# Score tiles of the maxima cut to 64 queries, the masked quarter left out, and the maxima turned by one transposition

## The reference

```python
# local attention: 16 heads of 16; a query sees only keys before it (distance 1..128)
allowed = (dist > 0) & (dist <= w) & (k_gpos >= 0)
scores = where(allowed, einsum('bhnqd,bhnkd->bhnqk', qb, kb) * scale, NEG)
local = softmax(scores) @ v            # rows with no allowed key give 0
# ... plus latent attention over 64 pooled tokens, a gate, and an output projection
# cross attention: 16 heads of 16, keys and values from ctx, causal (key <= query)
q, k, v = relu(query @ Wq + bq), relu(key @ Wk + bk), relu(value @ Wv + bv)
scores = where(tril, q k^T / sqrt(16), NEG)
out = layer_norm(softmax(scores) @ v + q) * gamma + beta
```

## Time and profile before

| | |
|---|---|
| median of three runs | 1628.79 us (1628.71 to 1629.89) |
| the profiled execution | 1626.49 us |
| its span, first to last instruction | 1624.8 us |
| PE busy | 1518.2 us (93%) |
| DVE, ACT, POOL busy | 1153.4 (71%), 931.4 (57%), 874.4 (54%) us |
| local attention, cross attention, slots | about 20 to 735, 735 to 1310, 1310 to 1625 us |

### The profile page before, as it was taken

The page is one execution under the profiler, slowest core; times in us unless marked ns, Lnnn a source line. Parts: engine busy times, 40 slices in busy tenths (PEclk is TensorE's granted clock), DMA queues, the critical chain, the costliest instruction groups (busy, mean ns, idle before and its releaser), DMA issues. The chain is left out here.

```text
span 1624.8 us, 50705 instructions
## 1 busy us (share of the span) xinstructions
PE 1518.2 (93%) x19038; PEld 1095.6 (67%) x19038; DVE 1153.4 (71%) x2897; ACT 931.4 (57%) x1542; POOL 874.4 (54%) x1178
## 2 busy tenths in 40 slices
PE   5999999999999999996999999999999958999997
PEld 3777777777777777764777777777777635666664
DVE  5767777777777777762676767676676737998986
ACT  2555555555555555543565666656566517777773
POOL 2455444555444554433466766767676633455553
PEclk8999999999999999997999999999999968999999
DMA  5400000000000000003000000000000000000001
GB/s 160 119 2 1 0 0 0 0 0 0 0 0 0 0 0 0 1 2 106 21 15 20 13 19 13 17 15 13 19 13 13 2 0 14 27 33 32 32 32 39
DMA packets 31200, 32.29 MB, mean 20 GB/s; under 512 B 3937, under 2 KB 29602, under 8 KB 31138
## 3 DMA queue, kind: packets, MB, share of 16 engines
q1 hardware_dynamic: 31138, 31.46, 6.2%
HBM read 23.06 MB, written 8.39 MB: 19 GB/s over the span
## 5 line engine op out<-in xcount | busy, mean ns | idle before, releaser
L1451 DVE TENSOR_REDUCE c_neg_max<-score_banks 128x16 f32<-128x2048 f32 x64 | 146.6, 2291 | 94.4 <-PE score_banks L1225 93.8
L980 POOL TENSOR_SCALAR_AFFINE_SELECT a_probs_t<-a_probs_t 128x512 f32<-128x512 f32 x256 | 161.9, 666 | 80.9 <-ACT a_probs_t L668 80.9
L994 POOL TENSOR_TENSOR a_less<-a_attn,a_remote 128x512 f32<-128x512 f32 x32 | 40.7, 1272 | 262.8 <-DVE a_attn L842 262.8
L1560 POOL TENSOR_SCALAR_AFFINE_SELECT c_probs_t<-c_probs_t 128x512 f32<-128x512 f32 x256 | 153.3, 635 | 26.6 <-ACT c_probs_t L1378 26.6
L822 DVE TENSOR_REDUCE a_neg_max<-score_banks 128x16 f32<-128x2048 f32 x64 | 146.4, 2287 | 20.9 <-PE score_banks L481 20.9
L668 ACT ACTIVATE a_probs_t<-score_banks 128x2048 f32<-128x2048 f32 x64 | 120.3, 1879 | 32.9 <-PE score_banks L513 32.9
L361 PE MATMUL side_banks<-a_xn_t,a_w_qk 128*128 128x256 f32 x512 | 131.9, 392 | 1.4 <-ACT a_xn_t L613 1.4
L1378 ACT ACTIVATE c_probs_t<-score_banks 128x2048 f32<-128x2048 f32 x64 | 120.3, 1880 | 13.5 <-PE score_banks L1253 13.5
L361 PEld LDWEIGHTS side_banks<-a_xn_t,a_w_qk 128*128 128x128 f32 x512 | 91.8, 194 | 10.8 <-ACT a_xn_t L613 1.8
L2063 POOL TENSOR_TENSOR r_hn<-rz_t,half_hn 128x256 f32<-128x256 f32 x32 | 23.4, 731 | 124.0 <-ACT rz_t L1895 124.0
L1571 POOL TENSOR_TENSOR c_scaled<-c_normed,gamma 128x512 f32<-128x512 f32 x32 | 40.6, 1270 | 91.6 <-DVE c_normed L1434 91.6
(11 more groups left out here) (254 smaller groups left out, 4136.8 us busy)
## 6 DMA issues: line engine op xcount, KB each, us to landing
x_sb<-in_x SPq DMA_DIRECT2D x32, 256.0 KB, 2.9
c_ctx_in<-in_ctx SPq DMA_DIRECT2D x32, 256.0 KB, 2.7
out<-y SPq DMA_DIRECT2D x32, 256.0 KB, 2.1
w_ih<-in_ffn_w_ih SPq DMA_DIRECT2D x1, 768.0 KB, 5.4
w_hh<-in_ffn_w_hh SPq DMA_DIRECT2D x1, 768.0 KB, 6.0
a_raw_qk<-in_attn_qk_w SPq DMA_DIRECT2D x1, 512.0 KB, 3.5
a_raw_cross<-in_xattn_qk_w SPq DMA_DIRECT2D x1, 512.0 KB, 4.6
b_ih<-in_ffn_b_ih SPq DMA_DIRECT2D x1, 384.0 KB, 6.7
```

Source lines behind the costliest of these rows:

```text
L980: nc.gpsimd.affine_select(out=probs, in_=probs, pattern=[[0, 4], [1, 128]], compare_op=ALU.is_ge, fill=0.0, base=-1, channel_multiplier=-1 ...
L1451: nc.vector.tensor_reduce(neg_max[:, tt, :], all_scores, AX.X, ALU.max, negate=True).then_inc(max_done, 1)
L1560: nc.gpsimd.affine_select(out=heads, in_=heads, pattern=[[0, 4], [1, 128]], compare_op=ALU.is_ge, fill=0.0, base=0, channel_multiplier=-1) ...
```

## The change

The four parts are the same in both attentions. **Scores for the maxima**: each 32x128 tile becomes two 32x64 tiles, one with queries 0 to 63 (`late` = 0) and keys 0 to 63, one with queries 64 to 127 and all 128 keys. The two heads of a matmul with `e` = 0 now lie on PSUM partitions 0 to 63 and those with `e` = 1 on 64 to 127, side by side, so that each bank uses 384 of its 512 columns. **Mask**: 8 matmuls on 64x64 tiles with 256 columns. **Maxima**: DVE reduces the two kinds of tile with one instruction each, over 512 and 1024 elements of a row. The 16 maxima and their remainders stand in 32 of 128 columns, so that one transposition turns them and a copy of 128x128 suffices. **Spread**: 16 matmuls with 128 columns each, of which each picks the row of its head by a 0/1 weight `slot_rows`, in place of 4 with 512 columns and ones.

```diff
@@ class CrossWeights: @@
-        self.mask = sb("mask_b", [128, 4, 128], BF16)
+        self.mask = sb("mask_b", [128, 128], BF16)
-        self.ones = sb("ones_b", [128, 128], BF16)
+        self.row_slot = sb("row_slot", [128, 4])
+        self.slot_rows = sb("slot_rows", [128, 4, 128], BF16)
@@ local_attention (cross_attention alike) @@
-    mask = sb("mask", [128, 4, 128], BF16)
+    mask = sb("mask", [128, 128], BF16)
-    max_part = sb("max_part", [128, 2, 4, 128], BF16)
-    max_t = sb("max_t", [128, 2, 512], BF16)
+    max_part = sb("max_part", [128, 2, 128], BF16)
+    max_t = sb("max_t", [128, 2, 128], BF16)
-    all_scores = score_banks[:].rearrange("p b n -> p (b n)").rearrange("p (h k) -> p h k", k=128)
+    all_scores = score_banks[:, :, 0:384].rearrange("p b (s k) -> p b s k", s=2)
@@ TensorE @@
+            def half(i):
+                return slice(64 * i, 64 * i + 64)
+            def near_far(rows, i):
+                return score_banks[rows, i, 0:384].rearrange("p (s k) -> p s k", s=2)
                 for i in range(4):
-                    for c in range(4):
-                        rows = group((i + c) % 4)
-                        pe.matmul(score_banks[group(c), i, :].rearrange("p (j k) -> p j k", j=4), ident_bf[rows, rows],
-                                  mask[rows, c, :].unsqueeze(1).to_broadcast([32, 4, 128]),
+                    for e in range(2):
+                        rows = half((i + e) % 2)
+                        pe.matmul(near_far(half(e), i)[:, :, 64:192], ident_bf[rows, rows],
+                                  mask[rows, :].unsqueeze(1).to_broadcast([64, 2, 128]),
                                   start=True, stop=False, skip_group_check=True)
-                toks = slice(S * tt, S * tt + S)
-                for e in range(2):
-                    for i in range(4):
-                        mm = pe.matmul(score_banks[:, i, 256 * e:256 * e + 256].rearrange("p (s k) -> p s k", s=2),
-                                       q_f[at.par][group(i), e, toks], k_z[at.par][group(i), e, :, toks],
-                                       start=False, stop=(e == 1), skip_group_check=True)
+                for late in range(2):
+                    for e in range(2):
+                        for i in range(4):
+                            mm = pe.matmul(near_far(half(e), i)[:, :, 128 * (1 - late):128 * (1 - late) + 64 * (1 + late)],
+                                           q_f[at.par][group(i), e, S * tt + 64 * late:S * tt + 64 * late + 64],
+                                           k_z[at.par][group(i), e, :, S * tt:S * tt + 64 * (1 + late)],
+                                           start=False, stop=True, skip_group_check=True)
@@ max_transpose @@
-                for j in range(4):
-                    mm = pe.transpose(maxT_bank[:].bitcast(BF16)[:, 128 * j:128 * j + 128], max_part[:, tt, j, :],
-                                      ident_bf[:])
+                pe.transpose(maxT_bank[:].bitcast(BF16)[:, 0:128], max_part[:, tt, :], ident_bf[:]).then_inc(maxT_filled, 1)
@@ scores_t @@
-                for i in range(4):
-                    mm = pe.matmul(score_banks[:, i, :], cross.ones[group(i), :], max_t[group(i), tt, :],
-                                   start=False, stop=True, skip_group_check=True)
+                for j in range(4):
+                    for i in range(4):
+                        by_row = score_banks[:, i, :].rearrange("p (e j r) -> p j e r", e=2, j=4)
+                        mm = pe.matmul(by_row[:, j], cross.slot_rows[group(i), j, :],
+                                       max_t[group(i), tt, :].rearrange("p (e r) -> p e r", e=2),
+                                       start=False, stop=True, skip_group_check=True)
@@ row_max @@
-                nc.vector.tensor_reduce(neg_max[:, tt, :], all_scores, AX.X, ALU.max, negate=True).then_inc(max_done, 1)
+                for late in range(2):
+                    ins = nc.vector.tensor_reduce(neg_max[:, tt, :].rearrange("p (i s l) -> p i s l", i=4, s=2)[:, :, :, late],
+                                                  all_scores[:, :, :, 128 * (1 - late):128 * (1 - late) + 64 * (1 + late)],
+                                                  AX.X, ALU.max, negate=True)
+                ins.then_inc(max_done, 1)
@@ max_parts @@
-                parts = max_part[:, tt, :, :].rearrange("p j (i u) -> p u i j", i=4)
+                parts = max_part[:, tt, :].rearrange("p (i u j) -> p u i j", i=4, j=4)
@@ copy_max: 128 columns in place of 512; set-up on DVE and POOL @@
+            nc.vector.tensor_copy(cross.slot_rows[:], cross.row_slot[:].unsqueeze(2).to_broadcast([128, 4, 128])).then_inc(zeroed, 1)
-            for r in range(4):
+            for r in range(2):
...
```

More of the change, by code:

```diff
@@ L931, in _ @@
             nc.vector.memset(lat_rows[:], 1.0).then_inc(zeroed, 1)
-            nc.vector.memset(cross.ones[:], 1.0).then_inc(zeroed, 1)
             dve.wait_ge(ident_made, 1)
@@ L937, in _ @@
                                     ALU.add).then_inc(rows_made, 1)
+            nc.vector.tensor_reduce(cross.row_slot[:], ident[:].rearrange("p (i r j) -> p j i r", i=4, j=4)[:, :, :, 0:2],
+                                    AX.XY, ALU.add).then_inc(rows_made, 1)
             x_scale(At(0, 0))
@@ L1216, in scores @@
                 for i in range(4):
-                    for c in range(4):
-                        rows = group((i + c) % 4)
-                        pe.matmul(score_banks[group(c), i, :].rearrange("p (j k) -> p j k", j=4), ident_bf[rows, rows],
-                                  cross.mask[rows, c, :].unsqueeze(1).to_broadcast([32, 4, 128]),
+                    for e in range(2):
+                        rows = half((i + e) % 2)
+                        pe.matmul(near_far(half(e), i)[:, :, 64:192], ident_bf[rows, rows],
+                                  cross.mask[rows, :].unsqueeze(1).to_broadcast([64, 2, 128]),
                                   start=True, stop=False, skip_group_check=True)
-                toks = slice(S * tt, S * tt + S)
-                for e in range(2):
-                    for i in range(4):
-                        mm = pe.matmul(score_banks[:, i, 256 * e:256 * e + 256].rearrange("p (s k) -> p s k", s=2),
-                                       q_f[at.par][group(i), e, toks], k_z[at.par][group(i), e, :, toks],
-                                       start=False, stop=(e == 1), skip_group_check=True)
+                for late in range(2):
+                    for e in range(2):
+                        for i in range(4):
+                            mm = pe.matmul(near_far(half(e), i)[:, :, 128 * (1 - late):128 * (1 - late) + 64 * (1 + late)],
+                                           q_f[at.par][group(i), e, S * tt + 64 * late:S * tt + 64 * late + 64],
+                                           k_z[at.par][group(i), e, :, S * tt:S * tt + 64 * (1 + late)],
+                                           start=False, stop=True, skip_group_check=True)
                 mm.then_inc(sc_filled, 1)
@@ L1235, in max_transpose @@
                     pe.wait_ge(maxT_ready, at.count(2, 1))
-                for j in range(4):
-                    mm = pe.transpose(maxT_bank[:].bitcast(BF16)[:, 128 * j:128 * j + 128], max_part[:, tt, j, :],
-                                      ident_bf[:])
-                mm.then_inc(maxT_filled, 1)
+                pe.transpose(maxT_bank[:].bitcast(BF16)[:, 0:128], max_part[:, tt, :], ident_bf[:]).then_inc(maxT_filled, 1)
             def scores_t(at, tt):
```

39 lines of the change are left out of this document (19 added, 20 removed).

## The result

The changed kernel takes 1576.02 us, the median of 4 runs (1572.53 to 1577.69), where the kernel before takes 1628.78 (the median of 4 runs, 1628.71 to 1629.89): a ratio of 0.9673, with a 95% interval of 0.9659 to 0.9688. The forecast was 1576. The profiled execution took 1575.13 us, with a span of 1573.4 us and a mean granted clock of 0.972 (before: 1626.49, 1624.8 and 0.976).

A forecast was written before the change was run, and what follows sets the result against it. TensorE was taken to bound both attention stages; 1.11 us a local step and 0.50 a cross step, times 32 each, gave 35.5 + 16 = 51.5 us off 1626.5, so 1575.0, median named 1576, range 1561 to 1600.

The forecast's parts named there:

- Scores and mask: TensorE, both attentions: scores 0.23 us less a call (1.07 to 0.84), mask 0.01 less (0.37 to 0.36).
- The bound of 0.80: Low bound in us for the scores of one call: all tiles side by side, with 0.16 of passage.
- rival 3: Scores and mask on TensorE: column halves take turns, +0.62 us a call, 1666 us in all; chance 0.06.
- Transposition and spread: TensorE, each call: one transposition in place of four saves 0.17 us; 16 spreads in place of four cost 0.015.
- Rival 4: TensorE: records start one after the other about every 25 ns, whatever their tile; 1613 us; chance 0.04.
- DVE's maximum: DVE, each call: two reductions of 1.22 and 0.69 us, 1.91 in place of 2.29, so 0.38 less.
- low bound of 1.76: DVE's two reductions of one call, in us, if the second hides its fixed part.
- arrive together: First turned scores, local attention: TensorE would come 0.97 us earlier with the stall, DVE 1.00, so 0.97 is gained.
- The stall: TensorE's wait for DVE's maximum before the first turned scores, local attention: 0.32 us a step to be regained.
- rival 1: Only local attention gains; POOL's chain or ACT's exp takes all of cross attention's saving; 1592 us; chance 0.12.
- Rival 2: Nothing absorbed: cross attention's first scores count too (8 us), scores and reductions at low bounds (4 us); 1564 us; chance 0.12.
- the wait in `values`: Cross attention, `values(old, 1)` waiting for POOL's mask: grows from 0.37 to 0.61 us a step, absorbing the first scores' 0.24.

The follow-up runs named there:

- e4: Changed kernel with the masked quarter computed and reduced too, same 32x64 tiles over all 128 keys: 1626.68 us, 0.9991 of the kernel before.
- e3: Changed kernel with one more DVE reduction of 512 elements of a row ahead of each maximum, both attentions: 1620.12 us, 0.9956 of the kernel before.
- e2: Kernel before with only the single transposition, 128x128 copy and 16 spreads; scores, mask and reduction as before: 1619.47 us, 0.9946 of the kernel before.
- e5: Kernel before with POOL's second mask in cross attention moved right behind the first, ahead of the two deviations: 1621.59 us, 0.9954 of the kernel before.
- e1: Changed kernel with maxima turned by four transpositions and spread by ones again, so only small tiles and missing quarter: 1593.57 us, 0.9790 of the kernel before.
- e6: Changed kernel with POOL's second mask in cross attention moved right behind the first, ahead of the two deviations: 1557.20 us, 0.9565 of the kernel before.

## Why the prediction was right, and where its terms were off

**The mechanism was right, step by step.** TensorE's own list sets the time of both stages, and the idle time at the turned scores in local attention went from 0.43 and 0.71 by turns to 0.33 and 0.34. Per local step 0.26 twice, 0.17 twice and the stall of 0.24, less 0.02 for the spreads, give 1.08, which is what was measured. In cross attention 0.26 for one call, 0.34 for the transpositions, less 0.02 and less 0.07 that goes to ACT's exp, give 0.51 against 0.52. That the median came out at the named 1576 to a tenth is luck: the four runs spread over 5 us, and the misses of the terms below partly cancel.

**Scores and mask.** Forecast 0.24 less a call, measured 0.26 (scores 1.07 to 0.83, mask 0.37 to 0.35). The bound of 0.80 lay under it. Eight 32x64 tiles do run side by side, and rival 3 (the column halves take turns, 1.48 us) fails: 32 records in 0.83 us. e4 adds what the prediction had not separated, that all of it is in the columns left out.

**Transposition and spread.** Forecast 0.17 less and 0.015 more, measured 0.17 to 0.18 and 0.01. Rival 4 (records start about every 25 ns) fails on the spread alone: 16 pairs and the passage take 0.33 us, where its 0.40 for the starts alone would show. The Trainium skill, "TensorE: Matmul & The Clock Gate", "Wait — 56ns, not 53.3ns?", gives that floor; by the rows above it does not hold between different tiles.

**DVE's maximum.** Forecast 0.38 less, measured 0.47 (1.82 us in place of 1.91, above the low bound of 1.76): the two overlap by 0.09 us. The prediction took all steps as alike and let both engines "arrive together" at the turned scores. That holds in every other step, where DVE's maximum ends 0.05 us ahead of them; in the steps between DVE has some 0.40 us to spare, and e3 shows what happens when that is used up. So the 0.09 had its worth: two maxima of 1.91 us would end 0.18 later, and by that estimate, which no run tests, every other step would be as much longer.

**The stall.** The mis-sized term, forecast 0.32 us a step. The total of 20.0 us in 31 waits holds one of 2.9 from the last step of the stage (it ends at 725.8 us), and in the middle the waits alternate. The timeline of the step that follows the one in the earlier trace rows has

```profile
437.57 0.98 PEld L509 LDWEIGHTS score_banks<-a_q_f,a_k_z 32*128 32x128 f32 x32 [0.43 <-DVE a_neg_max L822]
```

so the stall is 0.38 and 0.10 by turns, 0.24 in the mean. 0.08 too much here and 0.04 too little on two calls of scores and mask leave the 0.03 by which the local step was off.

**What the forecast did not see** is the place in cross attention where DVE's maximum ends 0.07 us before TensorE needs it. It had counted [0.33 <-DVE] in the earlier trace rows as nothing real to wait for, which is true of the time lost there, not of the margin. For the whole change it made no difference. DVE's second maximum starts when the scores end, so from there on only the transposition counts on TensorE's side: the turned scores come 0.17 us sooner behind the scores, and the maximum ends 0.47 sooner. The margin grew from 0.07 to 0.34, as DVE and PEld show after (970.48 to 970.82):

```profile
968.66 1.82 DVE L1475 TENSOR_REDUCE c_neg_max<-score_banks 128x8 f32<-128x512 f32 x2 [0.77 <-PE score_banks L1247]
...
970.82 0.98 PEld L1269 LDWEIGHTS score_banks<-c_q_f,c_k_z 32*128 32x128 f32 x32 [0.33 <-DVE c_neg_max L1475]
```

For every edit in this study that shortens TensorE's list ahead of the turned scores and leaves DVE's no shorter, it did matter: e2 and e5 gained less than expected for this reason, and e4 for the same one in both attentions. e1, which shortens DVE too, did not.

**Rivals 1 and 2.** Cross attention gained 0.52 a step, so rival 1 (nothing there) fails. Rival 2 (nothing absorbed) fails too, since the wait in `values` grew by 0.28 with the scores 0.26 shorter; e6 shows what it would have given had POOL's mask not stood behind the deviations.

## What to carry to other kernels

Before pricing a saving on the bounding engine, measure for each place where it waits for another engine not only the wait but the margin: the other engine's end against its own start. Where the margin is near zero, a saving counts only if both engines get shorter, and the two halves of a change can be worth less apart than together (here 42.8 against 51.9 us). A mean over a wait's total should be checked against two neighbouring steps, since one long wait at the end of a stage or an alternation hides in it; and a margin, like a wait, is to be compared between steps of the same kind. And where a saving disappears into a wait, look at what stands in the queue ahead of the late instruction: moving POOL's mask ahead of the work that it did not depend on gave 18.8 us more.

## What the runs showed of the hardware

Leaving columns out shortens small tiles, narrowing tiles does not: with all 128 keys, 32 records on eight 32x64 tiles took 1.05 us, and 16 records of as many columns each, on four 32x128 tiles, 1.07; with a quarter left out, 0.83.

Sixteen weight loads on 32x128 tiles took 0.34 us in all, with their 128-column matmuls beside them, and cost 0.01 us more than four loads with matmuls of 512 columns.

Two reductions in a row on DVE with nothing between them took 1.82 us where each alone shows 0.69 and 1.22.

One thing was not looked for. In e6 DVE's CAST of 16 elements a row, 0.17 us elsewhere, took 0.85:

```profile
977.37 1.27 POOL L1601 TENSOR_TENSOR c_shifted<-c_scaled,beta 128x512 f32<-128x512 f32 x1
...
977.82 0.85 DVE L1485 CAST c_max_part<-c_neg_max 128x16 bf16<-128x16 f32 x1
```

It ends at 978.67, 0.03 us after POOL's addition. In e5 the same operation took 0.52 and 0.43 us and ended 0.06 us after POOL's addition both times. The same holds in every step of the two runs: wherever the CAST starts during that addition (30 times in each), it ends 0.03 us after it in e6 and 0.06 in e5. It looks as if it had waited for POOL, but no run tests that by itself. TensorE didn't wait for it: the turned scores had started at 978.03.
